# A graph and cross-attention kernel: the norms' inverse deviation by logarithm and exponential, and new step orders

## What is computed

```python
# 1. LoRA experts with a router
logits = einsum('bsh,nh->bsn', x, router_W) + router_b;  w = softmax(logits)
a_sum  = einsum('bsh,arh->bsr', x, lora_A)               # lora_A is the context
y      = einsum('bsr,nhr->bsnh', a_sum, lora_B)
x      = nan_to_num(x + 0.5 * einsum('bsn,bsnh->bsh', w, y), 0.0, 1e4, -1e4)
# 2. cross attention, 32 heads of 16, then a norm over the 512 features
Q = x @ Wq.T + bq;  K = ctx @ Wk.T + bk;  V = ctx @ Wv.T + bv
attn = softmax(where(mask, Q K^T / 4, -inf));  x = x + (attn V) @ Wo.T + bo
mu, var = mean(x), mean((x - mu)**2)
x = (x - mu) / sqrt(var + 1e-05) * ln_g + ln_b
# 3. twice: a graph over 512 points (the context's columns), 4 blocks each
idx = top_8 nearest points
for i in range(4):
    p = leaky_relu(x);  c = w[i] @ p;  gn = w[i] @ gathered(p, idx)
    x = (c + gn.sum(over the 8)) / 9 + x
```

## Time and profile before

| | |
|---|---|
| time, median of 3 runs | 377.52 us (376.81 to 379.02) |
| span of the profiled execution | 378.0 us |
| TensorE busy, granted clock | 367.6 us (97%), 0.995 |
| VectorE busy | 272.0 us (72%) |
| ScalarE busy | 177.0 us (47%) |
| GpSimd busy | 129.0 us (34%) |

### The profile page before, as it was taken

One profiled execution on the slowest core, in us unless ns is written; L12 is line 12 of the kernel. 1 busy time (PEld: TensorE's weight loads), 2 busy tenths in 40 slices (PEclk: granted clock), 3 DMA queues, 4 the chain that ended last, 5 costly groups with the idle time before them and its releaser, 6 DMA issues.

```text
span 378.0 us, 6569 instructions
## 1 busy us (share of the span) xinstructions
PE 367.6 (97%) x2396; PEld 311.0 (82%) x2396; DVE 272.0 (72%) x427; ACT 177.0 (47%) x308; POOL 129.0 (34%) x125
## 2 busy tenths in 40 slices
...
GB/s 201 317 348 159 24 55 155 78 9 178 34 20 232 105 0 116 102 0 3 0 3 2 0 0 2 0 2 1 2 0 2 0 2 0 3 0 2 0 85 139
DMA packets 25056, 22.47 MB, mean 59 GB/s; under 512 B 9537, under 2 KB 20546, under 8 KB 25026
## 3 DMA queue, kind: packets, MB, share of 16 engines
...
q10 hardware_dynamic: 674, 0.02, 0.1%
...
## 4 chain that ended last, share of the span: by engine, by line
PE 85%; DVE 4%; ACT 4%; DMA 3%; issue 2%; SPq 1%; DVEq 0%; ACTq 0%
PE slot L564 82%; DMA wk<-in_WkT 3%; ACT k_blk_hi L943 2%; PE slot L684 1%; PE slot L693 1%; SPq L448 1%; PE slot L725 1%; ACT probT L976 1%; DVE p_full L1321 1%; DVE points L1331 1%; ACT adj L874 1%; DVE inv_full L1267 0%; ACT L976 0%; DVE stats L1282 0%; DVE shift L1255 0%
## 5 line engine op out<-in xcount | busy, mean ns | idle before, releaser
L1065 POOL TENSOR_TENSOR p_lo<-p_full,p_hi 128x512 fp32r<-128x512 f32 x64 | 86.0, 1362 | 157.1 <-ACT p_hi L1016 157.0
L1026 ACT ACTIVATE u_hi<-slot 128x512 fp32r<-128x512 f32 x64 | 36.2, 593 | 69.3 <-PE slot L564 69.0
L1326 DVE TENSOR_TENSOR u_lo<-slot,u_hi 128x512 fp32r<-128x512 f32 x64 | 42.4, 684 | 31.5 <-ACT u_hi L1026 31.5
L1016 ACT ACTIVATE p_hi<-p_full 128x512 fp32r<-128x512 f32 x64 | 39.0, 627 | 55.3 <-DVE p_full L1321 55.3
L564 PE MATMUL slot<-adj,u_hi 128*128 128x512 f32 x256 | 64.8, 392 | 0.1
L564 PE MATMUL slot<-fs_hi,p_hi 128*128 128x256 f32 x256 | 64.8, 286 | 0.0
L1331 DVE SCALAR_TENSOR_TENSOR points<-slot,points 128x512 f32<-128x512 f32 x64 | 42.7, 684 | 30.4 <-PE slot L564 30.4
L564 PE MATMUL slot<-adj,u_lo 128*128 128x512 f32 x256 | 64.1, 391 | 0.0
L564 PE MATMUL slot<-fs_lo,p_hi 128*128 128x256 f32 x256 | 64.1, 283 | 0.0
L1321 DVE SCALAR_TENSOR_TENSOR p_full<-points 128x512 f32<-128x512 f32 x64 | 54.3, 863 | 8.9 <-POOL p_lo L1065 6.3
L564 PEld LDWEIGHTS slot<-adj,u_lo 128*128 128x128 f32 x256 | 47.5, 188 | 10.1 <-issue 0.4
...
## 6 DMA issues: line engine op xcount, KB each, us to landing
...
```

The lines of the kernel that those rows point to most:

```text
L1016: act.activation(p_hi[b][:, (i % 2) * H:(i % 2 + 1) * H], p_full[:, p_buf[b, i]], ACT.Copy)\
L1026: act.activation(half_of(u_hi[:, u], i % 2), bank("wa", b, i // 2, i % 2), ACT.Copy)\
L1065: pool.tensor_tensor(lo[:, cut], full[:, cut], hi[:, cut].bitcast(F32), ALU.subtract)\
L1326: dve.tensor_tensor(half_of(u_lo[:, u], i % 2), bank("wa", b, i // 2, i % 2), half_of(u_hi[:, u], i % 2).bitcast(F32), ALU.subtract).then_ ...
```

## The change

The inverse deviation is computed on ScalarE as exp(-0.5 * ln(var + eps)), in place of a square root there and a reciprocal on VectorE; the second instruction waits for the first by a semaphore. A table set that holds logarithm and exponential is asked for ahead of ScalarE's steps. `ln` on VectorE loses its reciprocal. The unused kinds `rd`, `nm` and `pln` and what served them are gone. All five lists have the same steps as before in another order, TensorE's with other banks and u buffers.

```diff
@@ scalar engine
             act.dma_start(rb_all[:], router_b.unsqueeze(0).broadcast_to([P, NE])).then_inc(loads["rb"], 16)
+            act.preload_act_table_set("natural_log_exp_and_others")
...
                     after(act, var_ready, "st", b, 0)
                     after(act, var_ready, "st", b, 1)
-                    act.activation(dev[:, b], mean_var[:, b, :, 1], ACT.Sqrt, bias=eps[:]).then_inc(dev_ready, 1)
-                elif kind == "nm":
...
+                    act.activation(dev[:, b], mean_var[:, b, :, 1], ACT.Ln, bias=eps[:]).then_inc(act_step, 1)
+                    after(act, act_step, "dev", b)
+                    act.activation(rstd[:, b], dev[:, b], ACT.Exp, scale=-0.5).then_inc(rstd_ready, 1)
@@ vector engine
                 elif kind == "ln":
-                    after(dve, dev_ready, "dev", b)
-                    link(dve.reciprocal(rstd[:, b], dev[:, b]))
+                    after(dve, rstd_ready, "dev", b)
                     after(dve, centered, "ce", b, 0)
                     after(dve, centered, "ce", b, 1)
@@ PE_STEPS, before: the attention of all batches, the first layer units
-mb0:0 dist0_0:7 dist0_1:5 lora0:6 dist0_2:2 dist0_3:4 router0:0 keys:6,7 lora1:2 mixed0:0,1 router1:2 values:4,5
...
-w0_3:6,7 at0_0:0,1,5 at0_1 at0_2 at0_3 sc1_3:6,7 qa2:3,2 qb2 shift1:0 mixed3:6,7 norm0:4,5 qc2 sc2_0:0,1 rows0:5,4
-oa0 sc2_1:0,1 ob0 w1_0:2,3 oc0 sc2_2:6,7 w1_1:0,1 ua3:5,2 sc2_3:6,7 ub3 uc3 w1_2:6,7 shift2:5 at1_0:0,1,3 at1_1
-w1_3:4,5 at1_2 at1_3 rows1:7,4 qa3:2,6 qb3 norm1:0,1 qc3 wa0_0:2,3,0 wb0_0 sc3_0:0,1 wc0_0 wd0_0 oa1 sc3_1:0,1
-sc3_2:2,3 ob1 w2_0:0,1 oc1 w2_1:2,3 sc3_3:0,1 ga0_0:7,6 gb0_0 w2_2:2,3 at2_0:0,1,5 at2_1 gc0_0 gd0_0 w2_3:2,3
-shift3:7 at2_2 at2_3 rows2:2,7 wa1_0:4,6,1 wb1_0 wc1_0 wd1_0 norm2:0,1 wa0_1:5,3,0 wb0_1 wc0_1 oa2 wd0_1 ob2 oc2
-ga1_0:6,0 gb1_0 w3_0:4,5 gc1_0 gd1_0 w3_1:4,5 ga0_1:1,2 gb0_1 gc0_1 w3_2:6,7 at3_0:4,5,3 at3_1 dist3_0:0 w3_3:6,7
-gd0_1 at3_2 at3_3 wa1_1:1,6,1 wb1_1 wc1_1 adjT2:4,5 dist3_1:7 wd1_1 wa0_2:3,2,0 wb0_2 wc0_2 norm3:0,1 wd0_2 ga1_1:7,6
...
-gc0_7 ga2_7:3,4 gb2_7 gc2_7 gd2_7 wa3_7:5,6,1 wb3_7 wc3_7 wd3_7 wa1_7:2,3,0 wb1_7 wc1_7 wd1_7 ga3_7:1,5 gb3_7 gd0_7
-gc3_7 gd3_7 ga1_7:3,7 gb1_7 gc1_7 gd1_7
@@ PE_STEPS, after
+mb0:0 dist0_0:5 dist0_1:6 lora0:2 dist0_2:4 router0:7 dist0_3:0 keys:2,3 lora1:1 mixed0:0,4 values:6,7 router1:5
...
+dist2_3:7 qb1 qc1 shift0:4 ua2:6,5 sc1_2:0,1 ub2 sc1_0:2,3 uc2 w0_0:0,1 w0_1:6,7 lora3:3 sc1_1:4,5 w0_2:0,1
+at0_0:6,7,2 at0_1 w0_3:4,5 sc1_3:0,1 at0_2 at0_3 qa2:4,3 norm0:6,7 router3:1 qb2 qc2 shift1:0 rows0:6,7 oa0
+mixed3:0,2 sc2_2:4,5 ob0 oc0 sc2_0:2,3 ua3:1,0 ub3 w1_0:6,7 w1_2:2,3 w1_1:4,5 uc3 at1_0:6,7,5 at1_1 w1_3:0,1
+sc2_1:2,3 at1_2 at1_3 qa3:1,0 norm1:4,5 sc2_3:2,3 qb3 rows1:7,4 shift2:6 qc3 oa1 sc3_0:2,3 ob1 oc1 sc3_1:2,3
+wa0_0:6,5,0 sc3_2:0,1 wb0_0 wc0_0 sc3_3:2,3 wd0_0 ga0_0:1,0 gb0_0 w2_0:6,7 w2_1:4,5 gc0_0 w2_2:2,3 gd0_0 at2_0:6,7,5
+at2_1 w2_3:0,1 wa1_0:3,4,1 at2_2 at2_3 wb1_0 wc1_0 wa0_1:7,1,0 shift3:2 wb0_1 wd1_0 wc0_1 ga1_0:0,3 wd0_1 gb1_0
+norm2:4,5 gc1_0 gd1_0 ga0_1:6,4 gb0_1 gc0_1 w3_0:0,1 rows2:5,3 w3_1:6,7 gd0_1 w3_2:0,1 oa2 at3_0:6,7,4 at3_1 ob2
+w3_3:0,1 oc2 at3_2 at3_3 wa0_2:2,0,1 wb0_2 wc0_2 wd0_2 wa1_1:4,6,1 wb1_1 ga0_2:5,7 norm3:0,1 gb0_2 gc0_2 rows3:1,2
+wc1_1 gd0_2 wd1_1 oa3 ob3 ga1_1:4,0 gb1_1 gc1_1 oc3 gd1_1 adjT2:4,5 dist3_1:7 dist3_0:3 wa1_2:1,0,0 wa0_3:4,5,0
+dist3_2:6 wb1_2 wc1_2 wd1_2 dist3_3:7 wb0_3 wa2_0:2,3,1 wb2_0 wc0_3 ga1_2:1,7 gb1_2 wd0_3 gc1_2 gd1_2 wc2_0
...
+wa2_4:1,7,0 wd3_3 wb2_4 wc2_4 wd2_4 ga3_3:3,2 gb3_3 ga2_4:0,6 gb2_4 gc2_4 gd2_4 gc3_3 gd3_3 wa1_6:6,5,1 wa0_5:1,7,0
...
+gd2_5 wa3_5:7,2,1 wb3_5 ga0_6:5,3 wc3_5 gb0_6 wd3_5 ga3_5:4,0 gc0_6 gb3_5 gc3_5 gd3_5 gd0_6 wa2_6:5,4,1 wa1_7:0,2,1
+wa3_6:3,1,0 wb1_7 wb2_6 wc2_6 wb3_6 wd2_6 wc1_7 wc3_6 ga2_6:6,7 wd3_6 gb2_6 gc2_6 gd2_6 ga3_6:5,4 wd1_7 gb3_6 gc3_6
+gd3_6 wa0_7:1,6,1 wb0_7 ga1_7:5,3 gb1_7 gc1_7 wc0_7 gd1_7 wa3_7:5,4,0 wd0_7 wb3_7 wc3_7 wd3_7 ga0_7:2,1 wa2_7:7,0,1
+gb0_7 gc0_7 gd0_7 wb2_7 wc2_7 wd2_7 ga3_7:1,5 gb3_7 ga2_7:6,2 gc3_7 gd3_7 gb2_7 gc2_7 gd2_7
@@ DVE_STEPS, the starts
-mr fa a_ready fm init near0_0 rA0 near0_1 near0_3 near0_2 rB0 rA1 mk ml0_0 rB1 kl vr ml0_1 near1_0 ml1_0 raw0_0
+mr fa a_ready near0_0 fm near0_1 near0_2 rA0 rB0 near0_3 ml0_0 ml0_1 kl vr rA1 rB1 init raw0_0 nan0_0 raw0_1 ml1_0
@@ POOL_STEPS, the starts
-zb wql lbl zk wol ql0_0 ql0_1 zr ql1_0 ql1_1 ql2_0 ql2_1 diag0 diag1 pl0_0 pl0_1 ql3_0 ql3_1 pl1_1 pl1_0 pl0_2 pl0_3
+zr zb lbl wql zk wol ql0_0 ql0_1 ql1_1 ql1_0 ql2_1 diag0 ql2_0 pl0_0 pl0_1 diag1 ql3_0 ql3_1 pl1_0 pl1_1 pl0_2 pl0_3
```

More of the change, by code:

```diff
@@ L57 @@
-ga1_0:6,0 gb1_0 w3_0:4,5 gc1_0 gd1_0 w3_1:4,5 ga0_1:1,2 gb0_1 gc0_1 w3_2:6,7 at3_0:4,5,3 at3_1 dist3_0:0 w3_3:6,7
-gd0_1 at3_2 at3_3 wa1_1:1,6,1 wb1_1 wc1_1 adjT2:4,5 dist3_1:7 wd1_1 wa0_2:3,2,0 wb0_2 wc0_2 norm3:0,1 wd0_2 ga1_1:7,6
-gb1_1 gc1_1 gd1_1 ga0_2:2,0 gb0_2 gc0_2 gd0_2 wa2_0:6,1,1 wa1_2:7,3,0 wb1_2 wb2_0 wc1_2 wd1_2 wc2_0 rows3:0,2 oa3 ob3
-oc3 ga1_2:6,7 gb1_2 gc1_2 gd1_2 wd2_0 wa0_3:0,4,0 wb0_3 wc0_3 wd0_3 ga2_0:7,5 gb2_0 gc2_0 gd2_0 dist3_2:2 dist3_3:3
-wa1_3:6,1,1 wb1_3 wc1_3 ga0_3:5,4 wd1_3 gb0_3 gc0_3 gd0_3 adjT3:2,3 wa3_0:1,7,0 wb3_0 wc3_0 ga1_3:2,5 gb1_3 wd3_0
@@ L365, in xattn_graph_kernel @@
         wo_hi_ready = sem("wo_hi_ready")
[L366 to L367 removed]
+        act_step = sem("act_step")
+        rstd_ready = sem("rstd_ready")
         fs_hi_ready = sem("fs_hi_ready")
@@ L401, in loaded @@
             eng.wait_ge(loads[name], 16 * count)
-        def wait_ln(eng, b):
-            if b in POOL_LN:
-                after(eng, ln_pool, "pln", b)
-            else:
-                after(eng, ln_dve, "ln", b)
         def chain(eng, step):
@@ L611, in wait_read @@
                 elif kind == "rows":
-                    if b in POOL_LN:
-                        after(pe, normed, "nm", b, each=ST)
-                    else:
-                        after(pe, centered, "ce", b, part)
+                    after(pe, centered, "ce", b, part)
                 elif kind == "wa":
```

119 lines of the change are left out of this document (47 added, 72 removed).

## The result

The changed kernel takes 382.85 us (median of 4 runs, 381.71 to 383.88), the kernel before 378.27 beside it (376.81 to 379.30). The ratio is 1.0127, 95% interval 1.0095 to 1.0159: **slower by 1.3%, 4.8 us.** The prediction (375.7, range 373.4 to 378.6, slower 0.10) was wrong, in its sign too.

What follows compares the result with a forecast made beforehand. TensorE, busy for 97% of a 378.0 us span, was taken as the bound. Recovered 3.3 us and added 1.5 made -1.8; the same difference laid on the median of 377.52 gave 375.7 us, range 373.4 to 378.6.

Steps and rivals of the forecast that it cites:

- Start: ... Cost 0: Kernel start: VectorE's first neighbour step ahead of the context fill delays the fill to 13.9 us; cost 0, up to 1.5.
- Rival D: Layer stage: ScalarE's queue, held by high parts waiting for a u buffer, makes the kernel slower, 380.2 us; chance 0.10.
- Dead branches, a tile and semaphores go at no cost: no step used them.: Whole kernel: removing unused code, a tile and semaphores changes no time; cost 0.
- all new tight places together: Norms, ga0_0, wa0_3 and the layer stage: waits that the new orders add on TensorE, 1.5 us in sum.
- the whole 3.3 us: TensorE: time recovered from attention stalls, batch 2's transposes, norm3 and smaller gaps, 3.3 us in sum.
- If TensorE's idle time falls by 3 us and the span doesn't: Whole kernel: the sign, set beforehand, that the reading of TensorE's gaps is wrong; 3 us.
- between 0 and 1.4; I take 0: Start, at the keys: gain from TensorE work nearer to the keys keeping the clock; 0 to 1.4 us, taken as 0.
- the smaller 0.4: TensorE: smaller gaps recovered by the new orders, 0.4 us.
- the two stalls that the reading counted: Attention of batches 0 and 1: waits for ScalarE's exponentials go, 2 x 0.65 = 1.3 us.
- norm0 and norm1: Norms of batches 0 and 1: only 2.9 us of TensorE work ahead, 0.3 us lost at each, 0.6 in all.
- Rival E: Norms: logarithm and exponential are loaded apart, 8 loads, 10.3 us of ScalarE, giving 376.9 us; chance 0.06.
- Rival C: Whole kernel: stalls move, the new order losing 3.3 us at other places, giving 377.5 us; chance 0.16.

Runs made afterwards that it cites:

- e3: The changed kernel with the dropped 32-byte tile put back unused, so all addresses are as before; 380.91 us, 1.0082 of the kernel before.
- e5: e3 with ScalarE's sq2 moved behind the two high parts mh0_1 and mh0_0; 377.26 us, 1.0005 of the kernel before.
- e6: e5 with TensorE's lora3 put ahead of w0_0 and rows2 ahead of w3_0, to cover the row maxima's transfers; 377.22 us, 0.9988 of the kernel before.
- e2: The kernel before without the 32-byte tile and the unused branches naming it, old orders and norm; 379.85 us, 1.0062 of the kernel before.
- e1: The kernel before with the new norm alone, old orders, tile kept; 377.02 us, 0.9987 of the kernel before.
- e16: The kernel before with u moved 256 bytes further from adj, old orders; one run, no ratio, 512-column products 227 ns apart.

## Why the prediction was wrong

By ratios, which add up to the 0.0127 measured because each is a difference to the next. Their intervals are about 0.004 for the first two rows, 0.003 for the third and 0.002 for the last, so the last two can't be told from nothing:

| what | from | ratio |
|---|---|---|
| address of u | after less e3 | +0.0045 |
| sq2 at the front, with what the clock lost | e3 less e5 | +0.0077 |
| transfers of the row maxima | e5 less e6 | +0.0017 |
| norm, attention orders, the start, the rest | e6 | -0.0012 |

**Failed step 1: "Start: ... Cost 0".** The prediction followed VectorE's and TensorE's lists at the start and never ScalarE's. There the new list puts a step that waits for a batch-2 transfer ahead of a high part that batch 0 needs: 2.9 us. Rival D had the right form, ScalarE's queue held by one waiting step with work for TensorE behind it, but in the layer stage, where it did not happen: after 185 us TensorE is never idle.

**Failed step 2: "Dead branches, a tile and semaphores go at no cost: no step used them."** No step used the tile; its 32 bytes set the distance between `adj` and u. It costs 1.7 us by the ratios (e3 against after) and 2.3 alone (e2).

**Missing term: the row maxima's transfers.** w0_0 and w3_0 were moved towards their shift, and the wait for that DMA was in no term of the sum: 0.97 and 1.41 us, 2.4 in all in the trace, where 1.5 was put down for all new tight places together. What it costs in the median run is not shown: taking it away (e6) gives 0.6 us by the ratios and nothing by the medians.

**Failed reading, hidden by the rest: the gain itself.** The prediction put batch 1's stall down to the table loads and counted on the whole 3.3 us. e1 takes the loads away and the stall is still 0.36 us. And with every new stall mended (e6), TensorE's idle time from 20 to 185 us falls from 2.82 to 0.81 us, yet the runs' median is that of before. That is close to the prediction's own sign of a wrong reading ("If TensorE's idle time falls by 3 us and the span doesn't"). Whether other executions of e6 have waits that this trace lacks, or the gaps were priced too high, is open.

**Too small a term.** "between 0 and 1.4; I take 0" for the clock at the keys: e6 beside e16 shows 1.85 us in late executions.

**What held.** The sixteen attention steps take 17.65 us from start to start before, 16.62 with the norm alone (e1) and 15.11 after: 2.5 recovered in the traces, where 1.3 and part of the smaller 0.4 were forecast: besides the two stalls that the reading counted there were shorter ones, which a row that sums several products hides. rows2 and norm3 start with no wait, as forecast (0.97 and 0.65). norm0 and norm1, put at 0.6 us together, cost nothing; ga0_0 (forecast 0.1) is 0.3 late. wa0_3 (forecast 0.3) starts on time; the step ahead of it, wa1_2, loses 0.25 us instead, waiting for VectorE to read a bank of rows3, which was in no term. ScalarE's 7 loads of 1.28 us went and one stayed. Rival E is out: logarithm and exponential share a set. Rival C, that stalls move, holds in its form, but the stalls that came were larger than those that went. The reading that a load is worth only what waits behind it held twice over: 0.5 us with the old orders, 4.9 with the new.
